# A gating network's contraction in two row halves of the array, each half into its own PSUM bank, with the planner's rules changed to match

## The chip, the cores and the metric

One core of one Trainium2 chip runs the whole kernel in one launch. The metric is device time in microseconds (us), the median of 3 executions. The profile below is of one more execution.

## What is computed

The input `x` is 4 sequences of 2048 tokens, 256 features each, f32. It is layer-normalised (`xn`), and goes two ways.

```python
s = attention(xn)                  # 16 heads of 16; token i sees the keys j >= i
g = silu(network(xn))              # three layers of weights that are +1 or -1
return x + s * g

# network: [xn, -xn] (512) -> 1024 -> 1024 -> 256
h = relu(s0 * ([x, -x] @ w0)) * 2
h = relu(s1 * (h @ w1)) * 2
h = s2 * (h @ w2)
```

## The kernel before, in words

**Two stages.** `normalise_and_project` normalises, transposes and makes the queries, keys and values (up to some 180 us). `attend_and_combine` does all the rest, and the change is there.

**Work on TensorE (PE) in the second stage.** There are 16 groups, each 4 heads of one sequence, and each group has 40 steps of one block of 128 keys against up to 512 queries (512, 384, 256 or 128 near the diagonal). Operands that need more than one pass of precision are split in a high and a low part (`_hi`, `_lo`, type f32r).
- *Scores* ("S", L1288): two matmuls, one head in rows 0 to 63 of the array and one in rows 64 to 127, each into its own PSUM bank. ScalarE (ACT) takes the exponential of each bank (L1400).
- *Maxima* ("M", L1300): the same shape with the roles changed. VectorE (DVE) takes the row maximum of each bank (L1455, L1452). Scores of a step need the maxima of their queries.
- *Products* ("V" below, "PV" in the code, L1320): probabilities with values, four heads in four column quarters of the array, into a bank of their own. Each is f32 and shows as two records.
- *The network* ("F"): pieces of 256 tokens, 32 of them. L1339 is the first layer, L1342 the second, L1346 the third. Each matmul here has 128 rows, 128 columns of weights and 256 moving columns. In all there are 6144.
- *Others*: a transpose of the maxima (L1308) and the last projections (L1365, L1374, L1382), which use the whole array too.

So there are three ways to divide the array: whole (128x128), two row halves (64x128; S and M) and four column quarters (128x32; V). I call a pair of matmuls in the two row halves a row pair.

**Banks.** Seven banks (`BANKS`) are shared by S (2 each), M (2 each), the network and the others (1 each). `claimed` (used at each of these places) waits for the reader of the bank's last user.

**Network uses.** A *use* (`network_uses`) is a run of matmuls that fills one bank: a quarter of a first layer (8 matmuls), a quarter of a second (32), or a third layer (32). After a use ACT reads the bank (L1428, or L1420 and L1421), and GpSimd (POOL) splits the result (L1222, L1224). ACT may be two results ahead of POOL (`U_SLOTS`).

**What sets the order.** Every engine runs one list written out before the program is built, by `Plan`. It keeps an estimated clock for each engine and an estimated release time for each bank, and `choose` picks what TensorE does next: "R" (a row pair), "F" (network) or "V" (products). A change of division costs `ENTER`. Before the change, once in F it stays for `STRETCH` = 12 matmuls, and leaves for R only when `ENOUGH` banks are free or nearly so; in R it stays while two banks come free within `STAY` = 0.25 us. `network_behind` paces the network with the scores.

Of the kernel before, what the change touches and what calls it, by code (L numbers as in the profile page):

```python
# [14 lines left out]
P = 128  # L15
# [8 lines left out]
KH = H // P  # L24
# [28 lines left out]
USES = KF // FPU  # L53
# [493 lines left out]
def network_uses():  # L547

    out = []
    for k in range(PIECES):  # L550
        if k == 0:
            out += [("L0", 0, q, 8) for q in range(USES)]
        out += [("L1", k, q, 32) for q in range(USES)]
        if k + 1 < PIECES:
            out += [("L0", k + 1, q, 8) for q in range(USES)]
        out.append(("L2", k, 0, 32))
    return out

# [40 lines left out]
class Plan:  # L599
# [17 lines left out]
    def __init__(self):  # L617
# [10 lines left out]
        self.matmuls = self.begun = 0  # L628
# [48 lines left out]
    def beside(self, t):  # L677

        while self.side and self.side[0][0] < t:
# [3 lines left out]
            else:  # L683
                if what == "fetch" and self.due:

                    self.enter("F")
                    self.whole_array()
# [7 lines left out]
    def whole_array(self):  # L695

        while self.turns and self.turns[0][2] <= self.clock["PE"]:
            n, c, _ = self.turns.pop(0)
            self.end_span()
            at = self.emit("negmax", n, c)  # L700
# [4 lines left out]
        while self.due:  # L705
            self.end_span()
            event = self.due.pop(0)
# [6 lines left out]
    def network_behind(self):  # L714

        total = sum(use[3] for use in self.uses)
        lead = 28 * 11
        if self.scores == 0:
            return lead * min(1.0, self.maxima / (4 * LEAD)) - self.matmuls
        return lead + (total - lead) * min(1.0, self.scores / 2 / (TOTAL - FINISH)) - self.matmuls  # L720

    def network_from(self):

        if self.use == len(self.uses):
            return float("inf")
        if self.done > 0:
            return 0.0
        kind, k, q, _ = self.uses[self.use]
        start = min(self.release)
# [53 lines left out]
    def take_products(self):  # L783
# [3 lines left out]
        self.clock["PE"] += 4 * cols / self.STREAM  # L787
# [6 lines left out]
    def take_network(self, count):  # L794
        kind, k, q, total = self.uses[self.use]
        if self.done == 0:
            if kind == "L1" and q in (0, 2) and k + 1 < PIECES:
# [10 lines left out]
            self.take(("F", self.use), "f")  # L808
        bank = self.banks["F", self.use][0]
        count = min(count, total - self.done)  # L810
# [5 lines left out]
        self.clock["PE"] += 0.1177 * count  # L816
        self.matmuls += count
# [3 lines left out]
        if kind == "L2":  # L821
            self.release[bank] = self.reads("ACT", self.clock["PE"], self.EXP, 1400)
            self.clock["POOL"] = max(self.clock["POOL"], self.release[bank]) + 1.0
# [5 lines left out]
        else:  # L829
            if self.split >= U_SLOTS:  # L830
                self.clock["ACT"] = max(self.clock["ACT"], self.split_at[self.split - U_SLOTS])
            self.release[bank] = self.reads("ACT", self.clock["PE"], self.EXP, 640)
            self.clock["POOL"] = max(self.clock["POOL"], self.release[bank]) + 1.95
            self.split_at.append(self.clock["POOL"] + 0.1)
            self.split += 1
# [4 lines left out]
    def choose(self):  # L840
# [4 lines left out]

        late = behind > 0 and self.scores // 2 > TOTAL - STEPS
# [3 lines left out]
        if self.mode == "R":  # L850
            self.begun = self.matmuls
            if rows and pair <= now + self.STAY:
                return "R"
            if products and (waiting >= self.WAITING and not late or not network):
                return "V"
            return "F" if network else "V" if products else None
        free = sum(at <= now + self.SOON for at in self.release)
        if self.mode == "F":
            if network and (self.matmuls - self.begun < self.STRETCH or late):
                return "F"  # L860
            if rows and free >= self.ENOUGH["F"]:
                return "R"
            if products and waiting >= self.WAITING:
                return "V"
            if network:
                return "F"
        elif rows and free >= self.ENOUGH["V"]:
            return "R"
        if products:
            return "V"  # L870
        if network:
            self.begun = self.matmuls
            return "F"
        return "R" if rows and pair <= now + 0.4 else None
# [17 lines left out]
    def made(self):  # L892
        self.beside(-LEAD)
        while self.scores < 2 * TOTAL or self.products < TOTAL or self.use < len(self.uses):
# [7 lines left out]
            self.enter(kind)  # L902
# [11 lines left out]
            else:  # L914
                self.whole_array()
                self.take_network(2)
# [6 lines left out]
def attend_and_combine(nc, block, x, b_qkv, w_out, b_out, out, scratch, kept):  # L923
# [7 lines left out]
    pieces = pieces_in_order()  # L931

# [4 lines left out]
    with ExitStack() as ctx:  # L937
# [78 lines left out]
        f_ready, f_read = sem("f_ready"), sem("f_read")  # L1016
# [16 lines left out]
        def f_bank(use):  # L1033
            return ps[:, banks["F", use][0]].rearrange("p (t n) -> p t n", t=FPU)
# [151 lines left out]
        def _(pool):  # L1186
            pool.wait_ge(kept.through, COMPUTING)
            for what, *arg in order:
# [15 lines left out]
                elif what == "split_x":  # L1204
                    k, = arg
                    pool.wait_ge(x_loaded, (k + 1) * DMA)
                    if k > 0:

                        pool.wait_ge(f_ready, first_layer[k - 1] + 1)
# [3 lines left out]
                elif what == "F":  # L1213
                    use, split, need, k, kind, q, lo, hi, end = arg
                    if end and kind == "L2":
                        pool.wait_ge(f_read, use + 1)
                        pool.tensor_scalar(sig[:], sig[:], 1.0, 1.0, ALU.mult, ALU.add).then_inc(sig_added, 1)
                    elif end:
                        u_hi, u_lo = (u0_hi, u0_lo) if kind == "L0" else (u1_hi, u1_lo)
                        tiles = slice(q * FPU, (q + 1) * FPU)  # L1220
                        pool.wait_ge(f_read, use + 1)
                        pool.tensor_copy(u_hi[:, tiles], u[:, split % U_SLOTS]).then_inc(u_high, 1)  # L1222
                        pool.wait_ge(u_high, split + 1)
# [329 lines left out]
```

## Time and profile before

| what | value |
|---|---|
| median of 3 executions | 2429.61 us (2428.54 to 2431.49) |
| the profiled execution, its own time | 2430.44 us |
| its span, first to last instruction | 2428.7 us |
| PE busy | 2363.3 us (97%) |
| DVE busy | 1792.3 us (74%) |
| ACT busy | 1525.4 us (63%) |
| POOL busy | 913.9 us (38%) |
| mean granted TensorE clock | 0.989 |

Busy time counts an engine as busy while a record of it is open. Matmuls overlap in a pipeline, so the records of PE are longer than the time that one more matmul takes: that time is read from the distance between two starts in the timeline. Idle time of an engine that isn't the bound costs nothing.

### The profile page before, as it was taken

How to read it: one execution, taken by the hardware profiler on the slowest of the kernel's cores; microseconds unless marked ns; L12 is line 12 of the kernel's file. 1: busy time of each engine (PE TensorE's matmuls, PEld its weight loads, DVE VectorE, ACT ScalarE, POOL GpSimd, SP SyncE). 2: the span in 40 equal slices, each digit the busy share in tenths (PEclk: the TensorE clock that was granted, in tenths of full speed). 3: DMA queues.
4: the chain of work that ended last, by engine and by line, in shares of the span. 5: the costliest groups of instructions: out<-in, count | busy, mean ns of one | idle time of the engine just before them, and what ended most of it. 6: DMA issues, size and time to landing. Idle time of an engine off the chain costs nothing.

```text
span 2428.7 us, 50993 instructions
## 1 busy us (share of the span) xinstructions
PE 2363.3 (97%) x17616; PEld 1482.5 (61%) x17616; DVE 1792.3 (74%) x4516; ACT 1525.4 (63%) x3135; POOL 913.9 (38%) x1080
## 2 busy tenths in 40 slices
PE   7999999999999999999999999999999999999995
PEld 6777666656565656565655656566665666555652
DVE  7767777777777777777877777777777777777732
ACT  5664656667666676666666666666666666666552
POOL 1005334343333434343434434353434444344533
PEclk9999999999999999999999999999999999999997
DMA  8983112020111212131212112221212212122222
GB/s 307 353 326 112 37 33 58 24 64 23 45 39 43 77 53 78 39 87 39 82 46 74 55 39 76 56 79 41 77 44 68 63 37 83 49 73 78 62 72 81
DMA packets 157805, 192.67 MB, mean 79 GB/s; under 512 B 65276, under 2 KB 102076, under 8 KB 157560
## 3 DMA queue, kind: packets, MB, share of 16 engines
q1 hardware_dynamic: 156600, 189.41, 25.4%
q8 instruction: 152, 2.49, 0.4%
q14 instruction: 93, 0.76, 0.1%
q10 hardware_dynamic: 960, 0.00, 0.0%
HBM read 112.13 MB, written 76.14 MB: 78 GB/s over the span
## 4 chain that ended last, share of the span: by engine, by line
PE 90%; DMA 4%; DVE 2%; issue 1%; SPq 1%; ACT 1%; POOL 1%; POOLq 0%; ACTq 0%; DVEq 0%
PE b_ps L1342 22%; PE b_pv_ps L1320 22%; PE b_ps L1300 15%; PE b_ps L1288 15%; PE b_ps L1346 5%; PE b_ps L1339 5%; DMA a_xs<-L_attn_x 3%; PE b_ps L1365 3%; PE a_qk_ps L290 1%; DVE a_stats L396 1%; DVE a_qk_parts L434 1%; PE b_ps L1308 1%; PE a_v_ps L300 0%; ACT b_probs L1400 0%; SPq L1133 0%
## 5 line engine op out<-in xcount | busy, mean ns | idle before, releaser
L1400 ACT ACTIVATE b_probs<-b_ps 128x512 f32<-128x512 f32 (+3 forms) x2560 | 1184.1, 541 | 622.2 <-PE b_ps L1288 613.3
L1455 DVE TENSOR_REDUCE b_part_max<-b_ps 128x1 f32<-128x512 f32 x1536 | 960.8, 680 | 279.2 <-PE b_ps L1300 276.0
L1452 DVE CUSTOM_DVE_ANT_0 b_ps<-b_ps,k_mask 128x512 f32<-128x512 f32 (+3 forms) x1024 | 477.2, 518 | 214.3 <-PE b_ps L1300 212.7
L1320 PE MATMUL b_pv_ps<-b_probs,k_vst 128*32 128x512 f32 (+3 forms) x5120 | 583.7, 540 | 0.6 <-ACT b_probs L1400 0.5
L1342 PE MATMUL b_ps<-b_u_hi,k_w 128*128 128x256 f32 x2048 | 535.6, 298 | 0.0
L1288 PE MATMUL b_ps<-k_qst,k_kst 50*128 50x512 f32 (+3 forms) x2560 | 503.5, 411 | 7.2 <-ACT b_u L1428 3.7
L1300 PE MATMUL b_ps<-k_kst,k_qst 48*128 48x512 f32 (+3 forms) x2560 | 494.5, 410 | 3.3 <-DVE b_part_max L1455 0.9
L1342 PE MATMUL b_ps<-b_u_lo,k_w 128*128 128x256 f32 x2048 | 497.3, 279 | 0.0
L1342 PEld LDWEIGHTS b_ps<-b_u_hi,k_w 128*128 128x128 f32 x2048 | 386.7, 189 | 81.1 <-issue 72.2
L1300 PEld LDWEIGHTS b_ps<-k_kst,k_qst 48*128 48x128 f32 x2560 | 234.6, 185 | 299.4 <-issue 152.1
L1288 PEld LDWEIGHTS b_ps<-k_qst,k_kst 50*128 50x128 f32 x2560 | 244.9, 185 | 255.4 <-ACT b_probs L1400 84.7
L1222 POOL CAST b_u_hi<-b_u 128x512 fp32r<-128x512 f32 x256 | 157.9, 617 | 612.0 <-ACT b_u L1428 611.7
L1342 PEld LDWEIGHTS b_ps<-b_u_lo,k_w 128*128 128x128 f32 x2048 | 386.0, 188 | 0.4
L1224 POOL TENSOR_TENSOR b_u_lo<-b_u,b_u_hi 128x512 fp32r<-128x512 f32 x256 | 328.8, 1284 | 21.1
L1194 POOL TENSOR_SCALAR_AFFINE_SELECT b_probs<-b_probs 128x512 f32<-128x512 f32 x256 | 161.6, 634 | 356.2 <-ACT b_probs L1400 354.2
L1428 ACT ACTIVATE b_u<-b_ps,k_sign 128x512 f32<-128x512 f32 x256 | 175.4, 693 | 152.6 <-PE b_ps L1342 115.7
L1320 PEld LDWEIGHTS b_pv_ps<-b_probs,k_vst 128*32 128x32 f32 x5120 | 107.2, 108 | 157.7 <-issue 118.8
L1452 DVE DVE_READ_ACCUMULATOR2_ANT b_part_max<- 128x1 f32 x1024 | 143.5, 140 | 0.0
L1339 PE MATMUL b_ps<-b_x_hi,k_w 128*128 128x256 f32 x512 | 135.7, 299 | 1.1 <-POOL b_x_lo L1212 1.1
L1346 PE MATMUL b_ps<-k_w,b_u_hi 128*128 128x256 f32 x512 | 134.4, 299 | 0.0
L1339 PE MATMUL b_ps<-b_x_lo,k_w 128*128 128x256 f32 x512 | 126.3, 281 | 0.0
L1346 PE MATMUL b_ps<-k_w,b_u_lo 128*128 128x256 f32 x512 | 125.0, 281 | 0.0
(105 smaller groups left out, 1847.8 us busy)
## 6 DMA issues: line engine op xcount, KB each, us to landing
qk_parts<-a_qk_parts SPq DMA_DIRECT2D x64, 512.0 KB, 3.9
k_kst<-qk_parts SPq DMA_DIRECT2D x384, 64.0 KB, 2.3
k_qst<-qk_parts SPq DMA_DIRECT2D x384, 64.0 KB, 2.3
a_xs<-L_attn_x SPq DMA_DIRECT2D x16, 512.0 KB, 6.0
xn_T<-a_xT SPq DMA_DIRECT2D x16, 512.0 KB, 5.8
v_plain<-a_v_out SPq DMA_DIRECT2D x16, 512.0 KB, 5.6
k_xf<-xn_T SPq DMA_DIRECT2D x32, 256.0 KB, 3.2
b_v_in<-v_plain SPq DMA_DIRECT2D x64, 128.0 KB, 2.7
```

Source lines behind the costliest of these rows:

```text
L1194: pool.affine_select(out=at, in_=at, pattern=[[0, GH], [-1, P]], compare_op=ALU.is_ge, fill=0.0, base=0, channel_multiplier=1).then_inc(ma ...
L1224: pool.tensor_tensor(u_lo[:, tiles], u[:, split % U_SLOTS], u_hi[:, tiles].bitcast(F32), ALU.subtract).then_inc(u_split, 1)
L1288: pe.matmul(outs[half][:, 0:cols], keys, qst[rows, c, pair, 0:cols], start=True, stop=True).then_inc(s_ready, 1)
L1300: pe.matmul(outs[j], qst[rows, c, pair, i * P:(i + 1) * P], kst[rows, k_slot(kc, g % 2), pair, k1:CHUNK], start=True, stop=True).then_inc( ...
L1320: mm = pe.matmul(pv_ps[h * VW:(h + 1) * VW, 0:cols], vst[:, kb // TT, kb % TT, h, :], probs[:, s % P_SLOTS, h, 0:cols], start=start, stop= ...
L1339: mm = pe.matmul(dst[:, tile], kept.w0[:, f, m * P:(m + 1) * P], (x_hi, x_lo)[part][:, f, :], start=first, stop=last)
L1342: mm = pe.matmul(dst[:, tile], kept.w1[:, f, m * P:(m + 1) * P], (u0_hi, u0_lo)[part][:, f, :], start=first, stop=last)
L1346: mm = pe.matmul(dst[:, tile], (u1_hi, u1_lo)[part][:, f, tile * P:(tile + 1) * P], kept.w2[:, f, :], start=first, stop=last)
L1400: act.activation(probs[:, s % P_SLOTS, h, 0:cols], ps[:, banks[place, half][0], 0:cols], ACT.Exp, scale=HD ** -0.5).then_inc(exp_done, 1)
L1428: act.activation(u[:, split % U_SLOTS], f_bank(use), ACT.Relu, scale=kept.sign[:, layer:layer + 1]).then_inc(f_read, 1)
L1452: dve.tensor_tensor_reduce(src, src, mask[:, 0:CHUNK - k0 % CHUNK], 1.0, -3.0e38, ALU.add, ALU.max, dst).then_inc(ring_read, 1)
L1455: dve.tensor_reduce(dst, src, AX_X, ALU.max).then_inc(ring_read, 1)
```

## The change

A network matmul of 128 rows becomes two of 64 rows, issued one after the other as a row pair: in the first half of a use, rows 0 to 63 of the contraction go into bank 0 of the use and rows 64 to 127 into bank 1; in the second half they change places, so that each bank ends with both halves of its own tiles. Between the halves PE waits for its own last pair (`f_half`), since two row halves may not write one bank together. A use now fills two banks with 16 pairs (first layer), 64 (second) or 32 (third), there are 160 uses where there were 288, and the 6144 matmuls of 128 rows are 6144 row pairs. ACT reads and POOL splits both banks at the end of the use, one after the other, in the same sizes as before (the third layer's in two of 256 columns each).

In `Plan` the network is no longer a mode of its own: F and R share one division. It runs in quanta of 2 pairs, whenever no row pair can be issued, or when it is behind. `STRETCH`, `ENOUGH`, `STAY` and `SOON` are gone. V runs on until one step is left. The whole array is used for the transposes and projections alone, and these are placed where V begins or ends.

```diff
 FPU = 2
-USES = KF // FPU
+F_BANKS = 2
+USES = KF // (F_BANKS * FPU)
...
+def network_pair(kind, j):
+    depth = KH if kind == "L0" else KF
+    phase, at = divmod(j, (1 if kind == "L2" else FPU) * depth * SPLIT)
+    return phase, at // (depth * SPLIT), at // SPLIT % depth, at % SPLIT
...
-    STREAM = 2400.0
-    ENTER = {"R": 0.207, "F": 0.207, "V": 0.12}
+    STREAM, STREAM_V = 2200.0, 2360.0
+    PAIR = 0.1177
+    ENTER = {"R": 0.2, "V": 0.11, "W": 0.2}
...
-    ENOUGH = {"F": 5, "V": 4}
-    STRETCH, SLACK = 12, 40
-    STAY, SOON = 0.25, 0.6
-    WAITING = 4
+    WAITING, LEFT = 4, 1
+    SWAP = 0.45
+    SLACK, QUANTUM = 60, 2
...
+        if products and (waiting >= self.WAITING or self.mode == "V" and waiting > self.LEFT):
+            return "V"
+        if network and behind > 0:
+            return "F"
+        if rows and pair <= now:
+            return "R"
+        if network:
+            return "F"
+        if products and not (rows and pair <= now + 0.3):
+            return "V"
+        return None
...
-                        claimed(("F", use))
+                        for n in range(F_BANKS):
+                            claimed(("F", use, n))
...
+                        swapped, tile, f, part = network_pair(kind, j)
+                        if j == half_way:
+                            pe.wait_ge(f_half, use + 1)
+                        for n in range(F_BANKS):
+                            half = n ^ swapped
+                            rows = slice(half * HALF, (half + 1) * HALF)
+                            first, last = j == 0, swapped == 1 and f == depth - 1 and part == SPLIT - 1
+                            dst = f_bank(use, n)
+                            m = (q * F_BANKS + n) * FPU + tile
...
+                                mm = pe.matmul(dst[:, tile], w[rows, f, m * P:(m + 1) * P], x_parts[part][rows, f, :],
+                                               start=first, stop=last, skip_group_check=True)
+                            if end and j == hi - 1:
+                                mm.then_inc(f_ready, 1)
+                        if j == half_way - 1:
+                            mm.then_inc(f_half, 1)
```

**The order on PE, second layer, about a quarter of the way through the second stage.** Before, rows of L1342 are network matmuls, L1288 scores, L1300 maxima, L1308 the transpose:

```order
L1342 MATMUL b_ps<-b_u_hi,k_w 128x256
L1342 MATMUL b_ps<-b_u_lo,k_w 128x256
L1288 MATMUL b_ps<-k_qst,k_kst 128x512 x2
L1300 MATMUL b_ps<-k_kst,k_qst 128x512 x4
L1308 MATMUL b_ps<-k_identity,b_neg_max 128x128
L1342 MATMUL b_ps<-b_u_hi,k_w 128x256
L1342 MATMUL b_ps<-b_u_lo,k_w 128x256
L1342 MATMUL b_ps<-b_u_hi,k_w 128x256
```

Now, L1358 is the network, L1292 scores, L1304 maxima, and "x2" is one row pair:

```order
L1358 MATMUL b_ps<-b_u_lo,k_w 128x256 x2
L1292 MATMUL b_ps<-k_qst,k_kst 128x512 x2
L1358 MATMUL b_ps<-b_u_hi,k_w 128x256 x2
L1358 MATMUL b_ps<-b_u_lo,k_w 128x256 x2
L1358 MATMUL b_ps<-b_u_hi,k_w 128x256 x2
L1358 MATMUL b_ps<-b_u_lo,k_w 128x256 x2
L1304 MATMUL b_ps<-k_kst,k_qst 128x512 x2
L1358 MATMUL b_ps<-b_u_hi,k_w 128x256 x2
L1358 MATMUL b_ps<-b_u_lo,k_w 128x256 x2
L1292 MATMUL b_ps<-k_qst,k_kst 128x512 x2
```

Where scores and maxima stood in bunches between runs of 12 network matmuls, they now stand alone between runs of 2 to 8 network pairs, and no change of division lies between them.

**A place half way through another use, further on in the second layer on PE**, with the semaphores that a row waits for:

```order
L1358 MATMUL b_ps<-b_u0_lo,k_w1 128x256 x2
L1304 MATMUL b_ps<-k_kst,k_qst 128x512 [waits b_exp_done,k_k_loaded3,k_q_loaded2]
L1304 MATMUL b_ps<-k_kst,k_qst 128x512
L1358 MATMUL b_ps<-b_u0_hi,k_w1 128x256 [waits b_f_half]
L1358 MATMUL b_ps<-b_u0_hi,k_w1 128x256
L1358 MATMUL b_ps<-b_u0_lo,k_w1 128x256 x2
L1304 MATMUL b_ps<-k_kst,k_qst 128x512 [waits b_exp_done,b_ring_read]
```

One pair of maxima stands between the last pair of the first half and the wait for it.

## Rows read from the trace of the kernel before

**Rows 1.** The page's head: span, and busy time by engine.

```profile
span 2428.7 us, 50993 instructions
PE 2363.3 (97%) x17616; PEld 1482.5 (61%) x17616; DVE 1792.3 (74%) x4516; ACT 1525.4 (63%) x3135; POOL 913.9 (38%) x1080
```

**Rows 2.** The page's chain that ended last, by engine.

```profile
PE 90%; DMA 4%; DVE 2%; issue 1%; SPq 1%; ACT 1%; POOL 1%; POOLq 0%; ACTq 0%; DVEq 0%
```

**Rows 3.** Windows: length, busy us (count) of PE, PEld, DVE, ACT, POOL, clock, DMA.

```profile
200.00:2340.00 2140.00, 2127.80 (x16267) 1301.30 (x16269) 1623.61 (x4043) 1378.03 (x2869) 863.82 (x1019) 1.00 0.20 57
2340.00:2380.00 40.00, 37.07 (x264) 19.49 (x256) 6.61 (x13) 27.92 (x59) 18.30 (x20) 0.92 0.24 75
2380.00:2428.70 48.70, 24.10 (x96) 13.01 (x96) 13.59 (x17) 4.95 (x15) 12.80 (x13) 0.68 0.23 65
```

**Rows 4.** Timeline of PE, 1201 to 1206.5 us: start us, duration us, what.

```profile
1201.50 0.50 PE L1300 MATMUL b_ps<-k_kst,k_qst 48*128 48x512 f32 x2
1201.83 0.28 PE L1288 MATMUL b_ps<-k_qst,k_kst 50*128 50x256 f32 x2
1202.04 0.38 PE L1342 MATMUL b_ps<-b_u_hi,k_w 128*128 128x256 f32 x1
1202.27 0.28 PE L1342 MATMUL b_ps<-b_u_lo,k_w 128*128 128x256 f32 x1
1202.38 0.28 PE L1342 MATMUL b_ps<-b_u_hi,k_w 128*128 128x256 f32 x1
...
1203.40 0.28 PE L1342 MATMUL b_ps<-b_u_lo,k_w 128*128 128x256 f32 x1
1203.61 0.39 PE L1288 MATMUL b_ps<-k_qst,k_kst 50*128 50x256 f32 x2
1203.83 0.62 PE L1300 MATMUL b_ps<-k_kst,k_qst 48*128 48x512 f32 x4
1204.38 1.07 PE L1320 MATMUL b_pv_ps<-b_probs,k_vst 128*32 128x512 f32 x8
1205.37 0.50 PE L1288 MATMUL b_ps<-k_qst,k_kst 50*128 50x512 f32 x2
1205.71 0.48 PE L1300 MATMUL b_ps<-k_kst,k_qst 48*128 48x512 f32 x2
```

**Rows 5.** Timeline of PE: row pairs in the middle of a bunch, in three places.

```profile
218.65 0.22 PE L1288 MATMUL b_ps<-k_qst,k_kst 50*128 50x128 f32 x2
218.71 0.45 PE L1300 MATMUL b_ps<-k_kst,k_qst 48*128 48x512 f32 x2
...
793.50 0.39 PE L1300 MATMUL b_ps<-k_kst,k_qst 48*128 48x512 f32 x2
793.73 0.42 PE L1288 MATMUL b_ps<-k_qst,k_kst 50*128 50x512 f32 x2
...
1404.25 0.28 PE L1300 MATMUL b_ps<-k_kst,k_qst 48*128 48x256 f32 x2
1404.37 0.43 PE L1288 MATMUL b_ps<-k_qst,k_kst 50*128 50x512 f32 x2
```

**Rows 6.** Timeline of PE, 772 to 774 us: products of 128, 384 and 256 columns, merged.

```profile
772.19 1.50 PE L1320 MATMUL b_pv_ps<-b_probs,k_vst 128*32 128x128 f32 x24
773.62 0.44 PE L1288 MATMUL b_ps<-k_qst,k_kst 50*128 50x128 f32 x4
```

**Rows 7.** Timeline of DVE and ACT, 1201 to 1206.5 us: readers of row pairs.

```profile
1202.03 1.29 DVE L1455 TENSOR_REDUCE b_part_max<-b_ps 128x1 f32<-128x512 f32 x2 [0.53 <-PE b_ps L1300]
1205.96 1.09 ACT L1400 ACTIVATE b_probs<-b_ps 128x512 f32<-128x512 f32 x2 [1.28 <-PE b_ps L1288]
```

**Rows 8.** Groups of weight loads by shape: count, busy us, mean ns.

```profile
L1342 PEld LDWEIGHTS b_ps<-b_u_hi,k_w 128*128 128x128 f32 x2048 | 386.7, 189 | 81.1 <-issue 72.2 <-DVE b_part_max L1455 1.3 <-ACT b_probs L1400 0.7
L1288 PEld LDWEIGHTS b_ps<-k_qst,k_kst 50*128 50x128 f32 x2560 | 244.9, 185 | 255.4 <-ACT b_probs L1400 84.7 <-issue 62.8 <-DVE b_part_max L1455 35.8
```

More of the change, by code:

```diff
@@ L627, in __init__ @@
         self.use = self.done = self.split = 0
-        self.matmuls = self.begun = 0
+        self.pairs = 0
         self.needed, self.split_at = {}, []
@@ L718, in network_behind @@
         if self.scores == 0:
-            return lead * min(1.0, self.maxima / (4 * LEAD)) - self.matmuls
-        return lead + (total - lead) * min(1.0, self.scores / 2 / (TOTAL - FINISH)) - self.matmuls
+            return lead * min(1.0, self.maxima / (4 * LEAD)) - self.pairs
+        return lead + (total - lead) * min(1.0, self.scores / 2 / (TOTAL - FINISH)) - self.pairs
     def network_from(self):
@@ L807, in take_network @@
                     self.emit(*event[2:])
-            self.take(("F", self.use), "f")
-        bank = self.banks["F", self.use][0]
-        count = min(count, total - self.done)
+            for n in range(F_BANKS):
+                self.take(("F", self.use, n), "f")
+        taken = [self.banks["F", self.use, n][0] for n in range(F_BANKS)]
+        count = min(self.QUANTUM, total - self.done)
         lo, self.done = self.done, self.done + count
@@ L821, in take_network @@
         if kind == "L2":
-            self.release[bank] = self.reads("ACT", self.clock["PE"], self.EXP, 1400)
-            self.clock["POOL"] = max(self.clock["POOL"], self.release[bank]) + 1.0
+            for bank in taken:
+                self.release[bank] = self.reads("ACT", self.clock["PE"], self.EXP, 900)
+            self.clock["POOL"] = max(self.clock["POOL"], self.release[taken[-1]]) + 1.0
             t = self.step()
@@ L829, in take_network @@
         else:
[L830 to L835, printed above, removed]
+            for bank in taken:
+                if self.split >= U_SLOTS:
+                    self.clock["ACT"] = max(self.clock["ACT"], self.split_at[self.split - U_SLOTS])
+                self.release[bank] = self.reads("ACT", self.clock["PE"], self.EXP, 640)
+                self.clock["POOL"] = max(self.clock["POOL"], self.release[bank]) + 1.95
+                self.split_at.append(self.clock["POOL"] + 0.1)
+                self.split += 1
             self.needed["L1" if kind == "L0" else "L2", k] = self.split
@@ L844, in choose @@
         behind = self.network_behind()
-        late = behind > 0 and self.scores // 2 > TOTAL - STEPS
         network = self.network_from() <= now and behind > -self.SLACK
@@ L1348, in _ @@
-                    if end:
-                        mm.then_inc(f_ready, 1)
+                        swapped, tile, f, part = network_pair(kind, j)
+                        if j == half_way:
+                            pe.wait_ge(f_half, use + 1)
+                        for n in range(F_BANKS):
+                            half = n ^ swapped
[3 more added lines that the diff above has]
+                            m = (q * F_BANKS + n) * FPU + tile
+                            if kind == "L2":
+                                mm = pe.matmul(dst[:, 0], x_parts[part][rows, f, n * P:(n + 1) * P],
+                                               kept.w2[rows, f, :], start=first, stop=last)
+                            else:
+                                w = kept.w0 if kind == "L0" else kept.w1
+                                mm = pe.matmul(dst[:, tile], w[rows, f, m * P:(m + 1) * P], x_parts[part][rows, f, :],
+                                               start=first, stop=last, skip_group_check=True)
+                            if end and j == hi - 1:
+                                mm.then_inc(f_ready, 1)
```

118 lines of the change are left out of this document (47 added, 71 removed).

## The prediction

> **What bounds the kernel now.** I read the page's head first: PE is busy for 97% of the span, DVE for 74% and ACT for 63% [rows 1]. The chain that ended last then lies on PE for 90% [rows 2]. By stretches, in the 2140 us from 200 to 2340 PE is busy 2127.80 us, DVE 1623.61 (76%), ACT 1378.03 (64%) and POOL 863.82 (40%), and from 2380 on PE has half its time free [rows 3]. So over nine tenths of the kernel are PE's, and a reader should ask what PE does there besides streaming.
>
> The timeline shows it. A network matmul costs 0.11 to 0.12 us (1202.27 to 1202.38), 0.118 in the middle of the many. From the network to a row pair it takes 0.21 (1203.40 to 1203.61) and that pair of 256 columns 0.22 (to 1203.83) [rows 4], where inside a bunch such a pair costs 0.12 (1404.25 to 1404.37) [rows 5]: the change costs 0.09 + 0.10, say 0.20. Back again: 0.21 (1201.83 to 1202.04) in place of 0.12, and 0.23 (to 1202.27) in place of 0.12: 0.20 too [rows 4]. Products of 512 columns take 0.99 (1204.38 to 1205.37) [rows 4]; 768 columns take 1.43 [rows 6], so a column costs (1.43 - 0.99)/256 = 0.0017 us, 512 of them 0.88, and 0.11 is left for leaving. With 0.09 ahead of them (0.55 for two pairs of 0.23, 1203.83 to 1204.38) and 0.11 in the pair behind (0.34 for 0.23, 1205.37 to 1205.71) a visit to the columns costs some 0.32: I put 0.12 on going in and 0.20 on coming out [rows 4].
>
> Counted over the order, the array changes its division 2074 times in the second stage: 554 times into columns, 1520 times into halves or the whole. At these prices that is 554 x 0.12 + 1520 x 0.20 = 370 us. With it, and 0.118 for each of 6144 matmuls, 0.23 for 512 columns of a row pair and in proportion for less [rows 5], and 0.0017 a column for products, all of PE's work in the second stage comes to 2130 us, where the stretch took 2249 us. The 119 us between are waits. Some 39 of them lie after 2340, 7 before 200, and 73 in the 2140 us between.
>
> **The change, part by part.**
>
> *Fewer changes.* In the new order there are 1073: 470 into columns, 603 into the others. That saves 84 x 0.12 + 917 x 0.20 = 10 + 183 = **193 us**, all on the path, since PE is the bound there.
>
> *6144 matmuls become 6144 row pairs.* No row shows a row pair of this kernel that accumulates. The nearest are the pairs of scores and maxima of 256 columns, 0.12 a pair [rows 5], as a matmul of the whole array. I take 0.118, **no cost**. Both ends stand in the rivals.
>
> *Weights.* A pair has two loads of 128 columns. In the bunch at 218.65 a pair of 128 columns, with its two loads, takes 0.06 us [rows 5], half of what a network pair has. So the loads are hidden under 0.118, at no cost; without that cover they would be the bound (a rival).
>
> *The wait half way.* There are 160. In 159 of them other work stands between, in 54 one piece alone, mostly one pair of 512 columns. The last pair's record is 0.28 long [rows 4], and by 0.118 + 0.23 = 0.35 the next may start; I allow 0.06 for the signal, for 54 of them: **3 us**. Were nothing between, it would be some 0.3 for each of 160, 48 us.
>
> *ACT and POOL.* They do the same work. Two reads now come together, so a score behind them waits one read longer. POOL's two splits come together too, but a second-layer use is at least 64 x 0.118 = 7.5 us apart from the next. It shows in the banks.
>
> *Banks, what is late next.* This is the term that decides. The network holds two of seven banks for its whole use where it held one, and five are left: two row pairs and an odd bank. And the new rules issue a pair as soon as two banks are thought free, where the old ones kept bunches of 12 matmuls between. A row pair hands its second bank back so: maxima at 1201.50 are read from 1202.03 to 1203.32, 1.82 us later; scores at 1205.37 until 1207.05, 1.68 later [rows 4, 7]. Both pairs stood right behind a change of division, which lies in these distances with 0.10. I take 1.80 and 1.65 for the second bank, 1.18 and 1.10 for the first (a signal of 0.07 included), and less for shorter pairs. Then I summed PE's work between every use of a bank and the next. The middle distance falls from 2.28 us to 1.88. Before, 92 of 5501 hand-backs have less work between than the reader needs; now 768 of 5533. Paid in order (a wait that has been paid lengthens the distances behind it), the shortfalls come to 10 us before and to 103 us now, at 373 places of 0.28 each. So at least **93 us** of waits come in. These are the shortest hand-backs: a reader that still has another bank in front needs longer. The old order really waits 73 us in the middle. With 0.10 us more for each hand-back the two sums are 22 and 140, 118 more; with 0.25 more, 63 (about what was measured) and 231, 168 more. I take **118 us**, because pairs that stand alone queue less at their reader than bunches of three, and keep 93 and 168 as bounds.
>
> *The rest.* The first 180 us are untouched. The last 50 us, where PE is free for half the time [rows 3], stay as they are.
>
> Sum: 2430.4 (the profiled execution's own time, 0.8 above the median of the runs shown) - 193 + 118 + 3 = **2358 us**.
>
> **The rivals.**
>
> *The banks take back nearly all.* For it: DVE and ACT are not idle enough to be ignored (76% and 64% [rows 3]), and the 0.25 us that make the old sum match what was measured may hold for the new order too. Then 2430 - 193 + 168 + 3 = 2408, and up to 2430 if the queues grow with the share of the readers. Against it: the old waits come partly from bunches that are gone.
>
> *The waits don't grow.* If the readers were faster than I read, the whole gain stays: 2430 - 193 + 3 = 2240 at the bottom, 2300 if half of the waits come. Against it: 768 hand-backs shorter than the shortest read.
>
> *Slower: a pair of the network costs more than a matmul.* Mechanism: two row halves accumulate into two banks at once, with two loads of weights each 0.118 us, for runs of many pairs, and no row shows more than a few pairs in line. If one half had to wait for the other's load or write, a pair would cost up to 0.236: 6144 x 0.118 = 725 us more, 3083 us. It decides from (2430 - 2358)/6144 = 0.012 more, that is from 0.130 a pair. Against it: whole loads last 189 ns and those of 50 rows 185 [rows 8], yet a pair with two of them passes in 0.06 us [rows 5], so the two halves load side by side.
> The Trainium skill speaks for this rival ("TensorE: Matmul & The Clock Gate", "LDWEIGHTS (loading the stationary operand)"): a load takes its columns divided by 1.2, whatever its rows, so half the rows save nothing. By that figure, an estimate from the page, two loads one after the other are 213 ns a pair, 95 more than the pair streams, and the time would be some 2940 us. The rows agree that a load of 50 rows is no shorter, and the 0.06 us speak against loads in turn.
>
> *The change doesn't do what it says.* The division might depend on more than the halves, so that network pairs (64 rows) and scores (50) still pay. The new order has 2567 borders between the two; at 0.20 each that is 513 us: 2871. Against it: scores and maxima, 50 and 48 rows, stand side by side with nothing paid (0.06, 0.12, 0.23) [rows 5].
>
> **How the numbers follow.** A measurement of this kernel can tell about 0.2% (5 us) from no change. My forecast, waits of 93 to 150 more, has 0.70. The banks taking back nearly all has 0.14, of which 0.11 is still faster, 0.02 the same and 0.01 slower. Waits that don't grow have 0.05. The costlier pair has 0.08, 0.01 of it near no change and 0.07 slower. Borders that still pay have 0.03. That is 0.86 faster, 0.03 the same, 0.11 slower. The predicted time is the forecast's, 2358. For 8 in 10 I leave out the two slow cases and the bottom of the cheap one, and reach from 2300 to 2415: 2333 (the bound of 93) with room for rows of the order priced a little high, and the 2408 of the bound of 168.
>
> **What would show it.** Right: the distance from network pair to network pair 0.118, from network to scores and back the plain 0.118 and 0.23; PE's busy share in the middle falls below 97%, or, since its records are long and hide waits, starts of row pairs drift apart; ACT's and DVE's shares rise to some 66% and 79%. The waits of PE are at scores and maxima, for probabilities and maxima, not at the wait half way. Wrong: network pairs at 0.13 or more; 0.2 at borders between network and scores; a POOL split or ACT read as releaser of tens of us.

## The result, and the profile after

The changed kernel takes **2390.36 us** (median of 4 runs, 2388.42 to 2391.79) against 2430.18 for the kernel before (4 runs): ratio 0.9836, 95% interval 0.9819 to 0.9853. That is 40 us less, where 72 were forecast; 2390 lies inside the range of 2300 to 2415. The profiled execution took 2389.22 us.

The head of the page and its chain that ended last, by engine, answer to [rows 1] and [rows 2]:

```profile
span 2387.5 us, 63409 instructions
PE 2277.2 (95%) x23760; PEld 1558.8 (65%) x23760; DVE 1796.4 (75%) x4516; ACT 1541.1 (65%) x3199; POOL 913.9 (38%) x1080
...
PE 83%; DVE 5%; ACT 3%; DMA 3%; issue 3%; POOL 2%; SPq 1%; POOLq 0%; ACTq 0%; DVEq 0%
```

PE fell from 97% to 95% of the span, and its part of the chain from 90% to 83%; DVE and ACT, the readers of the banks, went from 2% and 1% to 5% and 3%. The same by stretches, columns as in [rows 3]:

```profile
200.00:2300.00 2100.00, 2046.91 (x22339) 1379.69 (x22335) 1629.77 (x4048) 1394.27 (x2933) 868.55 (x1024) 0.99 0.21 59
2300.00:2340.00 40.00, 34.86 (x288) 18.48 (x288) 7.79 (x13) 29.01 (x60) 14.35 (x14) 0.91 0.25 75
2340.00:2387.50 47.50, 23.06 (x84) 12.75 (x84) 13.64 (x17) 4.41 (x14) 12.61 (x12) 0.66 0.20 59
```

Two things stand there. PE has 53 us without a record in the 2100 us from 200 on, where it had 12 in 2140 [rows 3]. And the granted clock of this stretch is 0.99, where it was 1.00; that small number becomes a term below.

What PE does between two banks shows in its timeline (start, duration, what, and in brackets the idle time and its releaser); below it, ACT's for the same time:

```profile
1203.70 0.50 PE L1292 MATMUL b_ps<-k_qst,k_kst 50*128 50x512 f32 x2
1204.04 0.64 PE L1304 MATMUL b_ps<-k_kst,k_qst 48*128 48x512 f32 x4
1204.98 0.50 PE L1292 MATMUL b_ps<-k_qst,k_kst 50*128 50x512 f32 x2 [0.30 <-ACT b_probs L1414]
1205.41 1.06 PE L1324 MATMUL b_pv_ps<-b_probs,k_vst 128*32 128x512 f32 x8
1206.41 0.39 PE L1358 MATMUL b_ps<-b_x_hi,k_w 64*128 64x256 f32 x2
1206.63 0.28 PE L1358 MATMUL b_ps<-b_x_lo,k_w 64*128 64x256 f32 x2
1206.75 0.40 PE L1292 MATMUL b_ps<-k_qst,k_kst 50*128 50x512 f32 x2
1206.99 0.28 PE L1358 MATMUL b_ps<-b_x_hi,k_w 64*128 64x256 f32 x2
...
1202.84 1.09 ACT L1414 ACTIVATE b_probs<-b_ps 128x512 f32<-128x512 f32 x2 [0.22 <-PE b_ps L1292]
1204.24 1.09 ACT L1414 ACTIVATE b_probs<-b_ps 128x512 f32<-128x512 f32 x2 [0.31 <-PE b_ps L1292]
```

The border that the change set out to make free is free: network pair to score 0.12 us (1206.63 to 1206.75), score of 512 columns back to network 0.24 (to 1206.99), with no 0.09 and no 0.10 beside them. The other side stands at 1204.98: three row pairs (six of the seven banks) have gone out since 1203.70, the next finds no two banks free, and PE waits 0.30 for the exponentials that began at 1204.24.

PE's longest groups of waits (us in total, times, longest):

```profile
PE b_ps L1379 <- POOL b_heads_T L1258: 21.3, 4, 14.7
...
PE b_ps L1292 <- ACT b_probs L1414: 9.2, 23, 1.0
PE b_ps L1304 <- ACT b_probs L1414: 8.7, 26, 0.7
PE b_ps L1292 <- DMA k_qst<-b_max_parts: 8.0, 1, 8.0
```

These are only the gaps that outlast the records. For a full account I priced each piece of PE's second stage as the prediction did (distances without a wait: 0.118 a network pair, 0.455 us per 1000 columns of a row pair, 0.0017 a column of products, about 0.20 and 0.12 for a change of division), and took what the starts in the trace are further apart than that. From the first start of the stage to the last (the prediction's stretch of 2249 us ran to the end of the span, and its waits of 119 with it):

```
kernel            changes   PE's work   stretch   waits     time of the kernel
before             2074      2130        2244      114      2430.2
after              1073      1945        2204      259      2390.4
```

So work fell by 185 us and waits rose by 145. Of the 145, 56 stand in front of scores, 46 in front of network pairs, 40 in front of maxima and the rest in front of other pieces.

### The profile page after: what moved, and what is told of

The parts are those of the page before. It is cut to its first block, busy times and chain, and to the rows that moved or that the text cites. A ratio compares the mean times of both kernels' runs of the same rounds, so it can differ in the third digit from the quotient of the medians.

```text
span 2387.5 us, 63409 instructions
## 1 busy us (share of the span) xinstructions
PE 2277.2 (95%) x23760; PEld 1558.8 (65%) x23760; DVE 1796.4 (75%) x4516; ACT 1541.1 (65%) x3199; POOL 913.9 (38%) x1080
## 4 chain that ended last, share of the span: by engine, by line
PE 83%; DVE 5%; ACT 3%; DMA 3%; issue 3%; POOL 2%; SPq 1%; POOLq 0%; ACTq 0%; DVEq 0%
PE b_ps L1358 25%; PE b_pv_ps L1324 20%; PE b_ps L1292 13%; PE b_ps L1304 13%; PE b_ps L1354 5%; PE b_ps L1379 3%; DMA a_xs<-L_attn_x 2%; ACT b_probs L1414 2%; DVE b_part_max L1472 2%; PE a_qk_ps L291 2%; DVE b_ps L1469 1%; POOL b_u_lo L1228 1%; ACT b_u L1445 1%; PE a_v_ps L301 1%; DVE a_qk_parts L435 1%
## 5 line engine op out<-in xcount | busy, mean ns | idle before, releaser
L1292 PE MATMUL b_ps<-k_qst,k_kst 50*128 50x512 f32 (+3 forms) x2560 | 528.0, 406 | 31.7 <-ACT b_probs L1414 9.2
L1358 PE MATMUL b_ps<-b_u_hi,k_w 64*128 64x256 f32 x4096 | 551.0, 283 | 3.4 <-POOL b_u_lo L1228 1.3
L1358 PE MATMUL b_ps<-b_u_lo,k_w 64*128 64x256 f32 x4096 | 539.0, 277 | 0.0
L1304 PE MATMUL b_ps<-k_kst,k_qst 48*128 48x512 f32 (+3 forms) x2560 | 513.8, 399 | 20.5 <-ACT b_probs L1414 8.7
L1358 PEld LDWEIGHTS b_ps<-b_u_hi,k_w 64*128 64x128 f32 x4096 | 429.7, 187 | 28.2 <-DVE b_part_max L1472 8.1
L1358 PEld LDWEIGHTS b_ps<-b_u_lo,k_w 64*128 64x128 f32 x4096 | 429.5, 187 | 13.7
L1292 PEld LDWEIGHTS b_ps<-k_qst,k_kst 50*128 50x128 f32 x2560 | 260.5, 186 | 241.2 <-ACT b_probs L1414 82.9
L1304 PEld LDWEIGHTS b_ps<-k_kst,k_qst 48*128 48x128 f32 x2560 | 257.5, 186 | 197.4 <-issue 143.9
L1358 PE MATMUL b_ps<-b_x_hi,k_w 64*128 64x256 f32 x1024 | 149.8, 303 | 3.0 <-POOL b_x_lo L1213 1.5
L1358 PE MATMUL b_ps<-b_x_lo,k_w 64*128 64x256 f32 x1024 | 141.1, 285 | 0.0
L1354 PE MATMUL b_ps<-k_w,b_u_hi 64*128 64x256 f32 x1024 | 138.3, 284 | 1.0 <-issue 0.6
L1354 PE MATMUL b_ps<-k_w,b_u_lo 64*128 64x256 f32 x1024 | 133.8, 276 | 0.0
```

Source lines behind the costliest of these rows:

```text
L1292: pe.matmul(outs[half][:, 0:cols], keys, qst[rows, c, pair, 0:cols], start=True, stop=True).then_inc(s_ready, 1)
L1304: pe.matmul(outs[j], qst[rows, c, pair, i * P:(i + 1) * P], kst[rows, k_slot(kc, g % 2), pair, k1:CHUNK], start=True, stop=True).then_inc( ...
L1354: mm = pe.matmul(dst[:, 0], x_parts[part][rows, f, n * P:(n + 1) * P], kept.w2[rows, f, :], start=first, stop=last)
L1358: mm = pe.matmul(dst[:, tile], w[rows, f, m * P:(m + 1) * P], x_parts[part][rows, f, :], start=first, stop=last, skip_group_check=True)
```

## The experiments

The theory is the prediction's: the saved changes are real and cost nothing elsewhere on PE, and what is lost again is lost in waits for banks, because the network holds two of seven and row pairs follow each other too soon for their readers. The rivals: that the new rules of order alone bring the gain; that the half-way wait is what costs; that the waits do not come from how the order spaces the uses of a bank. In the whole section the kernel before took 2429.2 to 2429.3 beside the runs, and "work" and "waits" are reckoned as in the table above. Where no range is given there is one run; the four runs of one kernel lie 3 to 8 us apart, so a single one is good to a few us.

**Shorter readers, in either kernel.** The readers of scores and maxima read a quarter of the columns; exponentials and maxima of the rest are left out. The same edit in both:

```
-                        act.activation(probs[:, s % P_SLOTS, h, 0:cols], ps[:, banks[place, half][0], 0:cols], ACT.Exp,
+                        act.activation(probs[:, s % P_SLOTS, h, 0:cols // 4], ps[:, banks[place, half][0], 0:cols // 4], ACT.Exp,
...
-                        dst, src = part_max[ib // TT % 2][:, row, kc:kc + 1], filled((place, j))[:, 0:CHUNK - k0 % CHUNK]
+                        dst, src = part_max[ib // TT % 2][:, row, kc:kc + 1], filled((place, j))[:, 0:(CHUNK - k0 % CHUNK) // 4]
```

In the kernel before:

> The order of before, with readers that hand banks back early: ACT's exponential and DVE's maximum read only the first quarter of the columns of each bank of scores and maxima (three quarters of the exponentials and maxima are left out; the probabilities not written stay at a start value). Theory (changes of division and waits for banks are all that lies between the two kernels): the old order loses its 73 us of waits in the middle, so 2430 - 60 to 80 = 2350 to 2370. Rival (the waits have another source than the readers of these banks): within 20 us of 2430.

In the changed kernel:

> The same cut of the readers on the changed order (the same part is left out). Theory: nearly all of its 260 us of waits go, and the full 193 us of fewer changes of division shows between this run and the one with the order of before: 2160 to 2200, 160 to 195 below short_before. Rival (row pairs of the network cost something that is not a wait for banks): the two differ by about the 40 us that the kernels themselves differ by, 2310 to 2330 here.

Measured: 2415.84 and 2319.11. Both carry a wait that is the experiment's own, since GpSimd first fills `probs`, of which the exponentials now write only a part. It shows as the longest of this group of ACT's waits, 28.9 us, here in the changed kernel's version:

```profile
ACT b_u L1451 <- POOL b_u_lo L1233: 34.2, 5, 28.9
```

It holds PE for 28 us once, near 187 us. Without it they are 2388 and 2291. Waits are 73 us where the kernel before has 114, and 161 where the changed one has 259; work is the same. Reading time is therefore worth 98 us in the changed kernel and 41 in the one before. The direction is the theory's; the size is not: I had expected 190 or more to go in the changed kernel and 60 to 80 in the one before. The two runs differ by 97 us, where the theory said 160 to 195 and the rival (row pairs of the network cost something that isn't a wait for banks) some 40. The 2319.11 lies in the rival's range of 2310 to 2330, but with the experiment's own 28 us in it; without them it lies 19 below, and work, reckoned from the starts, has not grown. So neither expectation holds in full. The reads did get shorter by half:

```profile
L1420 ACT ACTIVATE b_probs<-b_ps 128x128 f32<-128x128 f32 (+3 forms) x2560 | 517.7, 261 | 1141.5 <-PE b_ps L1297 1136.4
```

261 ns against 539 with whole reads. But a hand-back also has a part that no shorter read removes: from the start of the pair to the reader's start (0.54 at 1203.70 to 1204.24 above), and the signal back. 89 us of the difference in waits between the two kernels stay (161 - 73, rounded) with readers that are idle for more than half of the time. That the order asks for banks back within that fixed part is how I read it; no run takes this part away. And not all of the 161 is such: the reads of the network's own banks were left as long as they were (686 ns each), and the waits of the last stretch, 39 us in the kernel before, are in it.

**One bank fewer, in either kernel** (`BANKS = 7` to `6`).

In the kernel before:

> The kernel before with six banks in the ring in place of seven, so that the network's one leaves five for row pairs, as after the change; all else, rules too, as before. Theory (five banks are too few): bunches break up, the order has 3005 changes of division where it had 2074 and hand-backs 95 to 125 us too short; priced work 2310 us in the second stage where it was 2130, waits 190 to 230: 2430 + 180 + 90 = 2700, 2660 to 2740 with the bounds. Rival (banks are not what counts): under 2500.

In the changed kernel:

> The changed kernel with one bank fewer for scores, maxima and network (BANKS 7 to 6). In the kernel before the same edit gave 3005 changes for 2074 and waits of 197 us for 114: there a shortage of banks is paid in changes first. Theory (in the changed kernel, where most borders cost nothing, a shortage is paid in waits): priced work only about 30 us more than the changed kernel's 1945 (1237 changes for 1073, and the network's two banks held as before), hand-backs short of the shortest latency sum to 215 us for 103, with a quarter of a microsecond added to the latency 376 for 231: waits of about 400 us for the 259 measured, so 2560 us, 2520 to 2610. Rival (the waits of the changed kernel come from elsewhere, the network's half-way change or its POOL work): waits hardly grow, 2400 to 2450.

Measured: 2688.97 and 2573.30. Before: 3005 changes, work 2306, waits 197, so 176 of the 259 us more are work. After: 1237 changes, work 1972, waits 415, so 156 of the 183 more are waits:

```profile
span 2571.6 us, 63410 instructions
...
PE 77%; ACT 8%; DVE 6%; DMA 3%; issue 3%; POOL 2%; SPq 0%; POOLq 0%; ACTq 0%; DVEq 0%
```

The chain now lies on the readers for 14%. A shortage of banks was paid for in changes of division before, and is paid for in waits now. That the changed kernel's waits come from elsewhere falls.

**The old rules with the new row pairs.** Bunches of 12 and the old thresholds choose what comes next, and the network is row pairs on two banks; the network goes first where it is behind.

```
-        if products and (waiting >= self.WAITING or self.mode == "V" and waiting > self.LEFT):
-            return "V"
...
+        free = sum(at <= now + self.SOON for at in self.release)
+        if self.kind == "F":
+            if network and (self.pairs - self.begun < self.STRETCH or late):
+                return "F"
+            if rows and free >= self.ENOUGH["F"]:
+                return "R"
```

> The changed kernel (row pairs, two banks a use) with the planner's old rules of choice (bunches of 12, ENOUGH, STAY, SOON), and one addition without which the network falls behind for good: it comes first when it is behind. Theory: only 1353 changes of division are left, so 149 us of priced work less than before (1981 for 2130), but the short hand-backs sum to 188 at the shortest latencies and 226 with 0.10 us more, where the changed order has 103 and 140: 2390 + 44 + 85 = 2520, 2480 to 2540. Then the row pairs alone, without the new rules, make the kernel slower. Rival (the rules of choice are a detail): 2390 to 2430.

Measured: 2560.54, just above the range; work 1991, waits 384. Row pairs with the old rules are 131 us slower than the kernel before. The waits are what makes them so; that they come from bunches of scores and maxima that meet banks of which the network now keeps two is the reading that the shortfalls of the expectation suggest.

**The new rules with the old network**, whole-array matmuls in one bank (the converse).

```
-    STRETCH, SLACK = 12, 40
+    STRETCH, SLACK = 12, 60
...
-    WAITING = 4
+    WAITING, LEFT = 4, 1
```

and the changed kernel's `choose` as it stands in the diff.

> The kernel before, its network still on the whole array and in one bank, but with the changed kernel's rules of what comes next and its constants WAITING, LEFT = 4, 1 and SLACK = 60. Theory (what the row halves bring is that a change between the network and scores or maxima costs nothing, and only this makes the new rules affordable): this order has 3462 changes of division instead of 2074, 1388 more at about 0.20 us, and products 271 times instead of 554 on a run of their own, so that priced work grows from 2130 us to 2431; few matmuls come to their bank too early (34 hand-backs short of the shortest latency, 7 us in all), so waits are about 50 to 85 us: 2700 us, 2660 to 2740. Rival (the rules alone bring the gain, the division of the network nothing): below the kernel before, 2390 to 2430.

Measured: 2682.63; work 2415, waits 82. In its timeline the border costs again what it did:

```profile
1204.69 0.40 PE L1272 MATMUL b_ps<-k_qst,k_kst 50*128 50x512 f32 x2
1205.02 0.38 PE L1323 MATMUL b_ps<-b_x_hi,k_w 128*128 128x256 f32 x1
1205.25 0.28 PE L1323 MATMUL b_ps<-b_x_lo,k_w 128*128 128x256 f32 x1
```

0.33 and 0.23 where the changed kernel has 0.24 and 0.12. Neither half of the change helps alone, each costs 130 us or more; the gain is in the two together.

**The places kept.** The half-way wait goes, and with it the change of places: each bank gets one half of the rows twice and the other never, so the network's sums are others.

```
-    if j == half_way:
-        pe.wait_ge(f_half, use + 1)
...
-    half = n ^ swapped
+    half = n
```

> The changed kernel without its half-way change of places: each half of the rows goes into its own bank for the whole use (so that each bank gets one half of its rows twice and the other never), and PE no longer waits half way. Order, pairs, loads and banks are the changed kernel's. Theory (the half-way wait costs next to nothing, since other work stands between in all but one of the uses): in the changed kernel's trace the pairs right behind the 160 half-way points start about 4 us later in sum than their work says, so 3 to 5 us less than the changed kernel's 2390: 2386, 2383 to 2389, some of which the waits for banks may take back. Rival (the half-way wait is what the growth of the waits hides in, since it holds two banks longer and every wait at a pair also exposes the next load): 20 us or more less, 2370 or below.

Measured: 2391.93 (4 runs, 2389.06 to 2396.92), ratio to the kernel before 0.9845 (0.9829 to 0.9861), the same as the changed kernel's. Waits are 259 us in both. The 4 us that were to be seen there did not come back, though the interval is some 4 us wide to either side. The rival's 20 us or more are out, and the wait at half way costs nothing that can be measured.

**Orders that space the banks.** Three tables for the changed kernel's planner, with the computation as it is. The first changes one line:

```
-    WAITING, LEFT = 4, 1
+    WAITING, LEFT = 5, 4
```

> The changed kernel with one line of the planner's table other: WAITING, LEFT = 5, 4 for 4, 1. Products of scores run in shorter runs, so that scores are taken back sooner and the readers of the banks are fed more evenly. In the order 1376 changes instead of 1073 (priced work 1984 us instead of 1937), hand-backs short of the shortest latency 239 for 373, summing to 49 us for 103; with a quarter of a microsecond more latency 160 for 231. Theory (the changed kernel gives back its saved changes in waits for banks, and the two can be traded): 47 us more work against 55 to 75 less waits: 2370 us, 2350 to 2395. Rival (waits are set by something other than the order's distance between a bank's taking and its retaking): 2430 or more, by the 47 us.

The second changes the planner's costs too:

```
-    STREAM, STREAM_V = 2200.0, 2360.0
+    STREAM, STREAM_V = 2200.0, 2355.0
...
-    ENTER = {"R": 0.2, "V": 0.11, "W": 0.2}
-    SEEN, FREED = 0.28, 0.18
-    EXP, MAX, MASKED_MAX = (1430.0, 0.119), (960.0, 0.065), (960.0, 0.2)
+    ENTER = {"R": 0.213, "V": 0.11, "W": 0.105}
+    SEEN, FREED = 0.284, 0.232
+    EXP, MAX, MASKED_MAX = (1269.2, 0.119), (960.0, 0.061), (960.0, 0.196)
...
-    WAITING, LEFT = 4, 1
+    WAITING, LEFT = 5, 4
...
-    SWAP = 0.45
+    SWAP = 0.319
...
-    AHEAD = 2
+    AHEAD = 1
+    URGENT, HOLD = 10, 0.192
...
-        if network and behind > 0:
+        if network and behind > self.URGENT:
...
-        if products and not (rows and pair <= now + 0.3):
+        if products and not (rows and pair <= now + self.HOLD):
```

> The changed kernel with its planner's costs and rules retuned: WAITING, LEFT = 5, 4; AHEAD 1; EXP's rate 1269 and FREED 0.232 (readers slower, as the traces show them); ENTER R 0.213 and W 0.105; SWAP 0.32; the network goes first only when it is over 10 pairs behind; products yield to rows that come within 0.19 us. The computation is the same. 1349 changes instead of 1073 (priced work 1980 us instead of 1937), hand-backs short of the shortest latency 145 for 373, 36 us for 103 in sum; with a quarter of a microsecond more 100 for 231. Theory (waits for banks follow from these distances): waits about 130 to 150 us for 259, so 2315 to 2345 us, 2330 likeliest, the fastest so far. Rival (waits don't follow): 2430.

The third is another set of the same kind:

> A second retuned table for the changed kernel's planner, found apart from the first: WAITING, LEFT = 5, 3; QUANTUM 1; AHEAD 4; SWAP 0.41; FREED 0.105; EXP (1310, 0.17), MAX (982, 0.11); the network goes first only when over 20 pairs behind; products yield to rows within 0.19 us. In the order 1308 changes (priced work 1973 us, 7 less than the first retuned one), hand-backs short of the shortest latency 227 for its 145, 54 us for 36 in sum, and 160 for 100 with a quarter of a microsecond more. Theory (work counted plus waits that follow from these sums): the waits of the versions run so far are 153 us at a sum of 100, 190 at 160, 259 at 231, so about 190 here: 1982 + 190 + 186 outside the contexts is 2358, 2340 to 2370, slower than the first retuned one by some 30 us. Rival (the sum of the shortfalls does not tell orders so close apart; the order's changes do): 2322, faster than the first by its 7 us.

Measured, with the others for comparison (shortfall: hand-backs with less work between than the shortest read plus a quarter of a microsecond, summed over the order):

```
kernel              changes  shortfall  work   waits   time      ratio to before
after                1073       231     1945    259    2390.4    0.9836 (0.9819 to 0.9853)
keep_products        1376       160     1994    190    2369.3    0.9758 (0.9742 to 0.9775)
retuned_b            1308       160     1983    180    2349.6    0.9668 (0.9652 to 0.9684)
retuned_a            1349       100     1990    153    2329.9    0.9593 (0.9579 to 0.9608)
six_after            1237       376     1972    415    2573.3    one run
```

The head and a window of the fastest, with the columns of [rows 3]:

```profile
span 2327.3 us, 63409 instructions
PE 2239.7 (96%) x23760; PEld 1493.0 (64%) x23760; DVE 1804.2 (78%) x4516; ACT 1540.6 (66%) x3199; POOL 910.1 (39%) x1080
...
200.00:2240.00 2040.00, 2003.24 (x22223) 1310.12 (x22222) 1637.29 (x4047) 1390.82 (x2925) 859.75 (x1019) 0.99 0.22 60
```

The forecasts from changes and shortfalls were 2370, 2330 and 2358. The fastest pays 276 more changes than the changed kernel, 45 us of work, and gets 106 us of waits back. It beats both kernels: 100 us less than before, 60 less than after. What the sum does not say is seen in retuned_b and keep_products, equal in shortfall and 10 us apart in waits. And the kernel before was not retuned in this way, so no run says how much a better order would have given it.

## Why the prediction was right, and where it was off

*Fewer changes, 193 us.* Right. Work fell by 185; the other 8 are a mis-sized piece. A transposition of the maxima used to have whole-array matmuls of the network behind it, which started 0.03 to 0.08 later. Now 62 of the 64 stand alone among row pairs and products, 0.26 each from start to the next piece's start, and with the changes around them they are 8 us dearer than I had priced them.

*6144 pairs at no cost; loads hidden.* Right: the middle one of 4795 distances from pair to pair is 0.118, and row pairs follow a network pair after 0.117. With it the costlier pair (which would have been 3083) and the borders that still pay (2871) are out. So the two loads of a pair are not paid one after the other, as the prediction's 2940 had it. The Trainium skill's rule for one load ("TensorE: Matmul & The Clock Gate", "LDWEIGHTS (loading the stationary operand)": its columns divided by 1.2, 107 ns for 128, whatever the rows) says nothing of two in turn; the prediction added that. The trace agrees that half the rows make a load no shorter (records of 187 ns for 64 rows in this trace, 189 for 128 rows in the one before), and not on the length itself, which is longer in the records than by the rule.

*The half-way wait, 3 us.* Nothing measurable (places_kept); small, as said.

*ACT and POOL.* As said: ACT 66% from 200 to 2300, DVE 78% (66% and 79% were named), and no wait of tens of microseconds behind POOL's splits.

*Banks, 118 us.* **This is the term that was mis-sized: 145**, inside the 93 to 150 of the forecast. The mechanism was right, as six_after and the three retuned orders show. The reason given for taking 118 of 93 to 168, that lone pairs queue less at their reader than bunches, no run tests. Three things were not in it:

First, one wait of 8.2 us behind the network pair at 2295.89, which has nothing to do with banks. Timeline of PE, DVE and SP's queue:

```profile
2295.89 0.28 PE L1358 MATMUL b_ps<-b_u_lo,k_w 64*128 64x256 f32 x2
2304.17 1.22 PE L1292 MATMUL b_ps<-k_qst,k_kst 50*128 50x512 f32 x4 [8.00 <-DMA k_qst<-b_max_parts]
...
2291.76 0.55 DVE L1505 RECIPROCAL b_sums<-b_sums 128x64 f32<-128x64 f32 x1 [6.22 <-DMA b_sums<-sums]
2292.48 0.28 DVE L1487 TENSOR_TENSOR b_max_parts<-b_ps,b_max_parts 16x128 fp32r<-16x128 f32 x1
...
2296.66 3.59 SPq L1134 DMA_DIRECT2D b_inv<-inv_sums  x8
2300.30 2.70 SPq L1075 DMA_DIRECT2D k_qst<-b_max_parts  x4
```

The last maxima were turned late. On DVE they stood behind a reciprocal that waited 6.22 us for its sums, and on SP, written at 2292.76, behind eight transfers that went out from 2296.66, so that they left at 2300.30.

Second, the clock. Windows of 20 us, the kernel before first, then the changed one:

```profile
2140.00:2160.00 20.00, 16.93 (x107) 9.94 (x108) 10.99 (x20) 11.28 (x26) 4.41 (x6) 0.83 0.48 144
```

```profile
320.00:340.00 20.00, 18.66 (x155) 11.38 (x155) 13.09 (x37) 13.46 (x25) 6.08 (x7) 0.83 0.22 55
620.00:640.00 20.00, 18.63 (x184) 10.58 (x183) 16.25 (x38) 9.56 (x26) 10.80 (x14) 0.88 0.12 34
...
1000.00:1020.00 20.00, 19.52 (x185) 12.56 (x179) 14.75 (x34) 15.04 (x31) 8.46 (x10) 0.91 0.11 28
```

Of the 105 windows from 200 to 2300 the kernel before has this one below full clock, the changed kernel twelve. The timeline of the last:

```profile
1002.47 0.99 PE L1304 MATMUL b_ps<-k_kst,k_qst 48*128 48x512 f32 x4 [0.39 <-ACT b_probs L1414]
...
1004.93 0.44 PE L1358 MATMUL b_ps<-b_x_hi,k_w 64*128 64x256 f32 x2
1005.14 0.44 PE L1358 MATMUL b_ps<-b_x_lo,k_w 64*128 64x256 f32 x2
...
1007.55 0.29 PE L1358 MATMUL b_ps<-b_x_lo,k_w 64*128 64x256 f32 x2
1007.67 0.30 PE L1358 MATMUL b_ps<-b_x_hi,k_w 64*128 64x256 f32 x2
```

A pair takes 0.21, at 1.2 GHz, and then 0.12 again, at 2.4. In the 12 us before the clock fell there, PE had waited 2.9 us in many pieces, none over 0.66. Starts in such stretches come 23 us later in sum than full clock would have them, against 7 before: 16 of the 145, an estimate, since the stretches have waits in them too. By the windows it is 18 (20 us x (1 - clock), summed: 21 in the changed kernel, 3 in the one before). This loss does not follow the sum of the waits: retuned_a loses 22 us with 153 us of waits (17 of them before 2240, where its last stretch begins), keep_products 14 with 190. In retuned_a the clock was low around single waits of 4.7 and 6.6 us, of which the changed kernel has none before 2295.

Third, a load that is no longer hidden. After a wait of over 0.1 in front of a score or maximum pair, what follows the pair in the same division is itself late, by 0.074 or more in nine of ten of 204 cases, at full clock; where there was no wait it is 0.003, the middle of 1380. Part of that lateness is the next bank's own wait, but the lower edge lies at 0.074 in the other versions too (340 cases of six_after). The Trainium skill says that PE's queue can pull a load of weights ahead of matmuls in flight ("TensorE: Matmul & The Clock Gate", "Architectural detail: the array is 16× 32×32, not 1× 128×128"). That fits: a load behind a waiting pair isn't pulled ahead. No run here takes the load away, so this reading is argued, not shown. Counting such waits from 0.05 up there are 471 for 198 before, and at that lower edge of the lateness 273 x 0.075 = 20 us go with it, an estimate. 8 + 16 + 20 leave 101 for the hand-backs alone, between the 93 of the shortest latency and the 118 taken. If this account holds, the hand-backs were priced a little too high, and what the prediction put at nothing, 44 us, is what made it come out short.

Sum: 2358 + 8 (transpositions) + 27 (145 for 118) - 3 (half way) = 2390.

*The rival that the banks take back nearly all* (2408 and up) was nearer to what came than its 0.14 suggests: the forecast lay 32 us below the result, that rival's bound 18 above.

## What to carry to other kernels

Work that costs nothing to put anywhere is placed wherever the planner likes, and the next scarce thing (here the banks) then sets the time: when a change removes a switching cost, retune the order for the resource that is short next. Here that was worth another 60 us on the 40 of the change itself. Before running an order, sum what its hand-backs fall short of the reader's latency; with the count of changes it gave the time of six new orders to 17 us or better (the last ones with the help of the waits of those run before), missed a seventh (old_rules) by 40 and the changed kernel itself by 32. And charge a short wait on PE with more than its length: what follows it starts late, and stretches of low clock came behind some of them.

## What the runs showed of the hardware

- Two row halves of 64 rows, accumulating into two banks in turn over the other's half, run at one whole-array matmul's pace: 0.118 us a pair of 256 columns over runs of many pairs. Halves of 64, 50 and 48 rows follow each other with nothing paid.
- Stretches at 1.2 GHz, in which a network pair takes 0.213 us instead of 0.118, came in the changed kernel from 200 to 2300 behind short waits only: before the one at 1003.9 PE had waited 2.9 us in pieces of at most 0.66. The kernel before has one such stretch from 200 to 2300, around one wait of 3.55 us. The clock lost there (20 us x (1 - clock), summed over the windows) is 3 us in the kernel before with its 114 us of waits, 9 in new_rules_whole with 82, 22 in retuned_a with 153, 14 in keep_products with 190, 21 in the changed kernel with 259, 81 in old_rules with 384 and 67 in six_after with 415: most where waits are most, but not in step with them.
- The way of a bank to its reader and back seems to have a fixed part: with reads of scores of 261 ns in place of 539, 161 of 259 us of waits stayed. The network's reads were not shortened in it.
